# Leaving out the short memset ahead of each of 1611 indirect gathers on GpSimd (graph layer and gated MLP, one core)

## The reference

```python
# layer 1
h = layernorm(x)
agg = segment_sum((h @ M)[src], dst)          # 200000 edges
x = x + relu(h @ W + agg)
# layer 2
h = layernorm(x)
scores = attention over 131072 edges of h @ W_gat, segment softmax, layernorm, mean of heads
w = softmax of the 2 best of 4 scores
x = x + sum_e gate[e] * (gelu(h @ W1[e] + b1[e]) @ W2[e] + b2[e])
```

## Time and profile before

| | before |
|---|---|
| median of 3 runs | 3524.27 us |
| the profiled execution, own time | 3527.7 us |
| its span, first to last instruction | 3526.5 us |
| mean granted TensorE clock | 0.883 |
| POOL busy | 2976.7 us (84%), 4438 instructions |
| PE busy | 2530.1 us (72%) |
| DVE busy | 2440.5 us (69%) |
| ring gathers L1746 | 1611, 1590.8 us |
| pauses L1725 | 2190, 780.5 us |

### The profile page before, as it was taken

One profiled execution on the slowest core, in us unless ns is written; L12 is line 12 of the kernel. 1 busy time (PEld: TensorE's weight loads), 2 busy tenths in 40 slices (PEclk: granted clock), 3 DMA queues, 4 the chain that ended last, 5 costly groups with the idle time before them and its releaser, 6 DMA issues.

```text
span 3526.5 us, 38735 instructions
## 1 busy us (share of the span) xinstructions
PE 2530.1 (72%) x10290; PEld 1713.0 (49%) x10315; DVE 2440.5 (69%) x5820; ACT 921.2 (26%) x1581; POOL 2976.7 (84%) x4438
## 2 busy tenths in 40 slices
PE   1555776768777777777877787778687877787725
PEld 1343455555554555545555565556454444443314
DVE  6677776777776556575555555555367988999957
ACT  3000111111112223211111111111144555555514
POOL 4888888888888888888888888888888888888841
PEclk9777898979888988878898899889899999999958
DMA  9676566666666666656666766666611222241147
GB/s 284 211 246 213 184 198 192 197 189 209 198 188 189 205 200 200 199 160 212 200 209 203 219 200 207 212 200 210 172 45 45 55 58 57 55 135 42 37 148 231
DMA packets 476794, 600.93 MB, mean 170 GB/s; under 512 B 72486, under 2 KB 415390, under 8 KB 474526
## 3 DMA queue, kind: packets, MB, share of 16 engines
q1 hardware_dynamic: 378766, 375.94, 32.7%
q0 software_dynamic: 97216, 219.88, 22.8%
q10 hardware_dynamic: 592, 2.64, 0.2%
HBM read 313.06 MB, written 286.79 MB: 170 GB/s over the span
## 4 chain that ended last, share of the span: by engine, by line
POOL 22%; DVE 22%; PE 12%; issue 8%; DMA 4%; another core or an unknown queue 1%; ACT 1%; DVEq 0%; SPq 0%; POOLq 0%; ACTq 0%
POOL ring L1746 16%; POOL pause L1725 6%; DVE picked L901 6%; DVE g L905 5%; PE wide L1645 4%; PE wide L1535 4%; DMA ring<-xn_d,srci 3%; DVE ring L855 2%; PE wide L1585 2%; PE wide L1595 1%; DVE one_hot L788 1%; DVE by_row L996 1%; DVE by_row L1003 1%; DVE comb L1178 1%
## 5 line engine op out<-in xcount | busy, mean ns | idle before, releaser
L1746 POOL DMA_INDIRECT ring<-xn_d,srci x1611 | 1590.8, 987 | 274.4 <-issue 194.5
L1535 PE MATMUL wide<-ring,one_hot 128*128 128x256 f32 x3222 | 963.8, 439 | 555.7 <-DMA ring<-xn_d,srci 493.4
L855 DVE SCALAR_TENSOR_TENSOR ring<-ring,same_v,wide 128x256 f32<-128x256 f32 x1610 | 773.2, 480 | 812.2 <-PE wide L1535 542.8
L1535 PEld LDWEIGHTS wide<-ring,one_hot 128*128 128x128 f32 x3222 | 682.4, 220 | 797.9 <-DMA ring<-xn_d,srci 548.5
L1725 POOL MEMSET pause<- 128x280 f32 x2190 | 780.5, 356 | 17.8 <-DVE ring L855 9.0
L1645 PE MATMUL wide<-tab_parts,low_hot 128*128 128x400 bf16 x3144 | 578.2, 338 | 151.7 <-DVE picked L901 107.7
L1790 POOL DMA_INDIRECT g<-tab_d,srt x500 | 495.8, 992 | 83.6 <-POOL pause L1725 50.0
L1645 PEld LDWEIGHTS wide<-tab_parts,low_hot 128*128 128x128 bf16 x3144 | 296.9, 99 | 428.3 <-issue 134.2
L788 DVE TENSOR_SCALAR one_hot<-iota_f,dloc 128x128 f32<-128x128 f32 x1611 | 457.7, 434 | 3.2
L1264 ACT ACTIVATE hh<-wide,b1c 128x512 f32<-128x512 f32 (+1 forms) x208 | 137.6, 662 | 1087.1 <-PE wide L1585 753.6
L1585 PE MATMUL wide<-xt,w1s 128*128 128x512 f32 (+1 forms) x832 | 417.4, 628 | 5.9 <-ACT hh L1264 2.6
(11 more groups left out here) (369 smaller groups left out, 1754.7 us busy)
## 6 DMA issues: line engine op xcount, KB each, us to landing
run_d<-ring SPq DMA_DIRECT2D x201, 1024.0 KB
ring<-xn_d,srci POOLq DMA_INDIRECT x1611
y_d<-yo SPq DMA_DIRECT2D x196, 128.0 KB
comb<-y_d SPq DMA_DIRECT2D x28, 896.0 KB
low_row<-low_d SPq DMA_DIRECT2D x13, 1024.0 KB
sum_d<-g SPq DMA_DIRECT2D x15, 768.0 KB
g<-tab_d,srt POOLq DMA_INDIRECT x500
xn_d<-ring SPq DMA_DIRECT2D x7, 896.0 KB, 7.1
```

Of the source, the lines that this page charges most:

```text
L855: dve_at["run", j] = step(V.scalar_tensor_tensor(out=o, in0=ring[:, (j - 1) // JC % RING, (j - 1) % JC, :], scalar=same_v[:, j:j + 1], in1 ...
L1535: mm = T.matmul(bank[pair_bank[p]][:, j % 2 * D:(j % 2 + 1) * D], one_hot[:, j // 4 % 4, j % 4, :], ring[:, j // JC % RING, j % JC, :], st ...
L1746: G.indirect_dma_start(out=ring[:, s, j % JC, :], out_offset=None, in_=xn_d, in_offset=at_rows(srci[:, j:j + 1])).then_inc(sem(f"gather{s} ...
```

## The change

The call of `pause_once()` ahead of each ring gather is left out, 1611 calls. The pauses ahead of all other indirect transfers stay, and so the function stands further down, ahead of `starts`.

```diff
-        pauses = itertools.count(1)
-
-        def pause_once():
-            n = next(pauses)
-            if n >= 2:
-                G.wait_ge(sem("paused"), n - 1)
-            G.memset(pause[:, :], 0.0).then_inc(sem("paused"), 1)
...
                 if j % 2 == 0 and j >= LEAD:
                     G.wait_ge(dve_step, dve_at["run", j - LEAD])
-                pause_once()
                 G.indirect_dma_start(out=ring[:, s, j % JC, :], out_offset=None, in_=xn_d,
                                      in_offset=at_rows(srci[:, j:j + 1])).then_inc(sem(f"gather{s}"), 16)
+
+        pauses = itertools.count(1)
+
+        def pause_once():
+            n = next(pauses)
+            if n >= 2:
+                G.wait_ge(sem("paused"), n - 1)
+            G.memset(pause[:, :], 0.0).then_inc(sem("paused"), 1)
```

## The result

The time did not fall: 3534.0 us in the median (3519.5 to 3553.3) against 3516.2 us of the kernel before beside it, a ratio of 1.0056, 95% interval [1.0041, 1.0072]. The forecast was 3254 us, in a range of 3140 to 3580. The range holds the time, but the change went the other way. The profiled execution has a span of 3539.0 us.

The account below looks back on a forecast made before the run. POOL's beat of ring gathers and pauses was taken to bound the first graph layer stage. Stage: 2014 + 90 + 72 = 2176 us instead of 2447, saving 271; 3527.7 - 271 = 3257, less 3.4: 3254 us, range 3140 to 3580.

Parts of the forecast that it names:

- The beat of POOL: Ring gathers of the first graph layer: without pauses they start 1.25 us apart instead of 1.463, gaining 0.213 us per visit.
- An engine that waits 12 us in 2447 for its consumers sets the pace itself: First graph layer stage: POOL waits 3.1 and 9.0 us for DVE's sums, so POOL sets the pace.
- The floor and the 90 us of disturbances: Same stage: 1611 x 1.25 = 2014 us at least, plus today's 90 us of longer gathers, pauses and waits kept.
- I allow ... 72 us: Same stage: waits for late sums, 0.06 us for 776 visits and 0.03 for 835, chosen rather than read.
- 1.27 of 1.31 us: PE's need per visit without its gather waits, against POOL's new time per visit; cover nearly gone.
- the slack of 4.8 us: Loop of 14 visits: room before a gather must wait for its sum, 4.8 us instead of 6.1.
- wrong ... if POOL waits 200 us for sums (PE): Sign against the forecast: POOL waiting 200 us for DVE's sums would mean PE had become the bound.
- The clock: PE's granted clock rises above 0.9 as idle time goes; 0.88 to 0.94 is worth 0.08 us per visit.
- The rest of the kernel: Everything after the first graph layer stage keeps its 1015 us.
- The port rival: Back-to-back gathers hold up DVE's `one_hot` comparisons at the shared port; run of about 4275 or 3775 us, slower 0.22.
- PE becomes the bound: PE's work plus waits for late sums sets the stage at 2275 us, half the gain; 3352 us, chance 0.13.
- the pause only fills idle time: Gathers under load need 0.2 us longer without a pause, beat stays 1.46; about 3524 us, chance 0.08.

Follow-up runs that it names:

- both kinds of occasion: Sessions on one chip with the kernel before timed beside: PE's completion signals came promptly in some, late in others; the kernel after took 3166.5 us or 3500.0 to 3544.8.
- `e_twice`: Kernel before with two pauses ahead of each ring gather instead of one: 4102.3 us (1.1718).
- `e_lead24p`: Kernel before, pauses kept, with LEAD 24 instead of 14: 3516.4 us (0.9988).
- `r_after3`: The kernel after, unchanged, run again where signals were prompt: 3166.5 us (0.9048) against the kernel before.
- occasions 2 and 3: Two follow-up sessions, signals held back in both; the kernel after, unchanged, took 3544.8 us (1.0068) and 3500.0 us (0.9974).
- the second kind: Sessions where PE's signals were held back: three of the five follow-ups and the one on which the result was measured (3534.0 us, 1.0056).
- occasion 4: Follow-up session with prompt signals: the kernel after, unchanged, took 3166.5 us (0.9048) against 3501.1 us of the kernel before.
- the first kind: Sessions where PE's signals came promptly, two of the five follow-ups; the kernel after took 3166.5 us (0.9048) on one of them.

## Why the prediction was wrong

**The beat of POOL: right.** 0.95 + 0.30 = 1.25 us, on both kinds of occasion.

**"An engine that waits 12 us in 2447 for its consumers sets the pace itself": right as far as it goes.** `e_twice` adds a pause and gets it in full, `e_lead24p` loosens the wait and gains nothing that can be told from none (0.9988, [0.9969, 1.0007]). It says what sets the pace now, and nothing of how much faster the consumers could go.

**The floor and the 90 us of disturbances: right in kind.** Where the signals are prompt, the stage takes 2173.5 - 63.7 = 2109.8 us. That is 96 us over the floor of 2014, where I had added 162.

**"I allow ... 72 us" for what is late then: the step that failed.** The term is the waiting for DVE's sums, forecast as 30 to 100 us on POOL. The waits measured 112.5 us in `r_after3` and 401.0 in the kernel after. They hold the 0.30 us that is idle ahead of every gather anyway, and one wait of 14.6 us behind the DVE instruction of 13.8 us, which in the kernel before was the gather of 14.24 us and so stands in the 90 us. An estimate of the term by itself is then 112.5 - 219 x 0.30 - 14 = 33 us in `r_after3`, and 401.0 - 268 x 0.30 - 14 = 307 us in the kernel after, where I had put 72. The whole stage of the kernel after lies 2462.6 - 2014 = 449 us over the floor, where I had added 162. Against `r_after3` it is 353 us longer, and POOL's idle time shows where: 289 us more behind DVE's sums and 62 more of "issue", for which the trace names no releaser.

I worked it out as a matter of how busy PE is (1.27 of 1.31 us), and held the slack of 4.8 us against "bursts" whose size I did not read. What fills the slack is the time from the end of a matmul to the start of the instruction that waits for it. In the trace of before this could be read: 80 late pairs of up to 4.9 us, 36 of them within 0.1 us of a recorded increment of PE, which a beat of 1.46 us leaves room for (its sums in the median started 5.4 us ahead of the gather that waits for them). At 1.25 us there were 285 of up to 8.3 us, with a median of 2.0 us left. That there would be more and longer ones at 1.25 us could not be read from it: the trace of before says only that such a delay exists. My own mark, "wrong ... if POOL waits 200 us for sums (PE)", was met, but its cause was not PE's work: PE is busy 293 and 315 us of the two stretches, as in the earlier trace rows.

**The clock: right where prompt only.** The kernel after has 0.88 and 0.91, against 0.87 and 0.89, since PE's idle time did not go. `r_after3` from 400 to 800 us, the columns as in the earlier trace rows, has 0.93:

```profile
400.00:800.00 400.00, 321.60 (x1259) 237.59 (x1258) 323.01 (x877) 73.71 (x109) 298.80 (x295) 0.93 0.71 224
```

**The rest of the kernel:** 1012.5 us in the kernel after, as forecast 1015; 993 in `r_after3`.

**The rivals.** The port rival is refuted: `one_hot` fell from 457.7 us to 363.4. It is the pauses that hold the comparisons up, and the more the wider they are: the mean of one is 303 to 304 ns without pauses, 311 with pauses of 8 elements, 327 of 140, 434 and 439 of 280 (428 with two of them per gather). The Trainium skill (SBUF — State Buffer, section "SBUF: two separate sides") has the loser of the shared port blocked for the whole of the other's instruction. The trace doesn't agree for the gathers: beside gathers of 0.95 us without pauses no comparison in the kernel after is longer than 0.53 us, against 0.27 for the shortest. "PE becomes the bound" and "the pause only fills idle time" named 3352 and 3524 us. The second came nearest to the number and is wrong in its mechanism, as the beat did fall to 1.25. None of the three has late signals in it, so the chance of 0.22 for slower was given to a cause that does not exist here, and it was luck that a range drawn up to 3580 us for these rivals held the time.

**What is settled, and what is not.** Settled: the change takes 0.21 us from each gather and was worth 9.5% on the one occasion on which it met prompt signals; on occasions 2 and 3 and on that of the result the same program ran into late signals, which ate the gain. On the occasions of the second kind the number of late pairs goes with the beat (79 or 80 at 1.46 us, 237 to 250 at 1.35 to 1.36 in the mean, 260 to 285 at 1.25), and the longest came with LEAD 24; neither a short instruction between the gathers nor even spacing removes them. Not settled: what holds the signals back, and what makes an occasion of one kind or the other. It does not go with the chip: chip 9 was of the second kind on occasion 2 and of the first on occasion 4. One thing goes with it throughout: on the second kind the trace itself lacks records. Of the 806 increments that PE makes for pairs of visits, it holds 591 to 646 there and 801 to 807 on the first kind; of all semaphore records 21 to 30 thousand instead of 59 to 62 thousand. Whether recording takes part in the lateness, or both come from one cause outside the kernel, no run here tells: every timed execution has a granted clock on record, so there seems to be none without recording to compare with. The Trainium skill (NOTIFIC — Programmer's Manual, section "When the ring fills") says that in the default mode a full queue loses the new record and only in another mode blocks the engine. The missing records agree with the first; late signals would need something more than it.

## What to carry to other kernels

A waiting time near zero says who sets the pace today, not how much room the others have. Before you price a faster producer, read from the trace how long its consumers' signals take (end of the matmul to start of what waits for it, the longest and not only the median) and set that against the slack of the loop. And when variants of one kernel do not fall in line, run the disputed one together with those that surprised you: here the occasion was worth 290 to 490 us to kernels with dense gathers and about 20 us to the kernel before, which made it look like a property of the change.

For this kernel: no pause with LEAD 24 is best where signals are prompt (0.8956) and worst where not (1.0314); a pause of half the width was faster on either kind (0.9503, 0.9937).

## What the runs showed of the hardware

- PE's completion signals can come 8 to 10 us (16 us with LEAD 24) after the matmul, several at once and in PE's own order (9.9 us for one `hh` of the kernel after, its increment recorded at 2244.32). In all eight traces of the other kind of occasion, the same program among them, they are recorded within 0.1 us of the matmul's end, but for at most 6 of 806. The durations on DVE and ACT are the same on both.
- A memset of 128x8 float32 between two indirect gathers costs nothing in the beat (1.26 us instead of 1.25): it fits in the 0.30 us that is idle anyway; 128x140 costs 0.10 and 128x280 0.21 us.
- The memsets, more than the gathers, are what stretches DVE's comparisons (267 ns at least; in the mean 303 ns with gathers alone, 434 with 128x280 ahead of each gather).
